# Expert matmuls over the 64 lower and the 64 upper output partitions, as two instructions each

## What is computed

```python
def body(acc, ws):
    wgu, wd, we = ws
    gu = x @ wgu                       # (tokens, 256) @ (256, 192)
    gate, up = jnp.split(gu, 2, axis=-1)
    act = jax.nn.silu(gate) * up       # (tokens, 96)
    out = act @ wd                     # (tokens, 96) @ (96, 256)
    return (acc + we[:, None] * out, None)
init = jnp.zeros_like(x)
final, _ = lax.scan(body, init, (gate_up_weights, down_weights, combine.T))
```

## Time and profile before

| what | value |
|---|---|
| time, median of 2 runs | 538.03 us (535.09 and 540.96) |
| span of the profiled execution | 534.3 us |
| TensorE busy | 478.1 us, 89% of the span |
| TensorE loads busy | 388.2 us, 73% |
| VectorE / ScalarE / GpSimd busy | 66% / 62% / 45% |
| chain that ended last | 61% TensorE, of it L1474 14%, L1494 9% |

### The profile page before, as it was taken

How to read it: one execution, slowest core, us unless ns; L and a number is a source line. 1 busy time by engine, 2 the same in 40 slices (tenths; PEclk the granted TensorE clock), 3 DMA queues, 4 the chain that set the end, 5 groups by cost and what they waited for, 6 DMA issues and landing times.

```text
span 534.3 us, 10363 instructions
## 1 busy us (share of the span) xinstructions
PE 478.1 (89%) x2751; PEld 388.2 (73%) x2751; DVE 352.2 (66%) x1175; ACT 332.2 (62%) x1021; POOL 238.5 (45%) x255
## 2 busy tenths in 40 slices
PE   3886999999989799999998647999999999999875
PEld 1466767887778777778875636889999898999621
DVE  5868488487398489479679744856666665666432
ACT  4556786888676879777987813555555555555400
POOL 0354102011012571101577777767667676765700
PEclk9899999999999999999999859999999999999989
DMA  7930992000030220300277246999999999993497
GB/s 274 421 130 20 301 334 85 1 1 1 2 80 10 73 76 10 76 2 0 82 269 275 91 150 187 368 400 399 400 393 388 397 396 398 385 366 131 150 354 250
DMA packets 71560, 108.54 MB, mean 203 GB/s; under 512 B 10234, under 2 KB 49351, under 8 KB 71120
## 3 DMA queue, kind: packets, MB, share of 16 engines
q1 hardware_dynamic: 62336, 90.93, 48.3%
q0 software_dynamic: 9168, 16.95, 8.7%
HBM read 81.31 MB, written 34.77 MB: 217 GB/s over the span
## 4 chain that ended last, share of the span: by engine, by line
PE 61%; DVE 14%; ACT 12%; DMA 6%; issue 4%; SPq 2%; POOL 1%; POOLq 0%; DVEq 0%; ACTq 0%
PE ps L1474 14%; PE ps L1214 10%; PE ps L1494 9%; PE ps L1339 7%; ACT lg L634 4%; DVE lg L912 3%; ACT lg L577 3%; PE ps L1262 2%; PE ps L1210 2%; PE ps L1212 2%; PE ps L1211 2%; PE ps L1255 2%; SPq L414 2%; PE ps L1320 2%; PE ps L1327 2%
## 5 line engine op out<-in xcount | busy, mean ns | idle before, releaser
L563 POOL DMA_INDIRECT pair_rows<-eout,dest x127 | 126.0, 992 | 54.9 <-DVE dest L1185 42.2
L1474 PE MATMUL ps<-wts,xg 128*128 128x192 f32 x508 | 105.0, 330 | 0.0
L1474 PEld LDWEIGHTS ps<-wts,xg 128*128 128x128 f32 x508 | 80.8, 193 | 0.1
L774 ACT ACTIVATE sact<-ps 128x96 f32<-128x96 f32 x127 | 31.9, 251 | 75.8 <-PE ps L1474 75.8
L1494 PE MATMUL ps<-wts,aT 96*128 96x256 f32 x254 | 76.0, 381 | 0.0
L1182 DVE COPY xg<-ps 128x256 f32<-128x256 f32 x127 | 53.9, 424 | 29.0 <-PE ps L1214 28.5
L634 ACT ACTIVATE lg<-lg,mneg 128x128 f32<-128x128 f32 (+1 forms) x128 | 56.4, 442 | 26.1 <-DVE mneg L912 26.1
L1195 DVE SCALAR_TENSOR_TENSOR aact<-sact,xrow,ps 128x96 f32<-128x96 f32 x127 | 39.9, 314 | 48.1 <-ACT sact L774 47.7
L483 POOL DMA_INDIRECT slot_rows<-rows,pair_slot x48 | 48.1, 1002 | 32.9 <-DVE hit L977 20.1
L577 ACT ACTIVATE eout<-ps 128x256 f32<-128x256 f32 x127 | 48.8, 384 | 17.2 <-PE ps L1494 1.2
L1214 PE MATMUL ps<-ident,xrow 128*128 128x128 f32 x254 | 50.1, 278 | 9.5 <-DMA xrow<-slot_rows 9.5
(11 more groups left out here) (220 smaller groups left out, 1043.3 us busy)
## 6 DMA issues: line engine op xcount, KB each, us to landing
wts<-in_experts_dram SPq DMA_DIRECT2D x127, 320.0 KB
xrow<-slot_rows SPq DMA_DIRECT2D x127, 130.0 KB, 7.9
slot_rows<-zero SPq DMA_DIRECT2D x1, 8320.0 KB, 28.3
pairs<-pair_rows SPq DMA_DIRECT2D x16, 512.0 KB
wT<-in_wq_t_dram SPq DMA_DIRECT2D x4, 512.0 KB, 6.8
wq_raw<-in_wq_l_dram SPq DMA_DIRECT2D x1, 2048.0 KB, 14.9
wo_sb<-in_wo_l_dram SPq DMA_DIRECT2D x1, 2048.0 KB, 20.7
bm<-bias_rows SPq DMA_DIRECT2D x4, 512.0 KB, 3.5
```

The lines of the kernel that those rows point to most:

```text
L563: nc.gpsimd.indirect_dma_start(out=pair_d, out_offset=bass.IndirectOffsetOnAxis(ap=dest[:, t:t + 1], axis=0), in_=eout[t % NOUT][:], in_of ...
L1474: ins = nc.tensor.matmul(ps[:, 2 + u % 2, 0:I2], xg[u % 3][:, cc, :], wts[u % NBUF][:, cc * I2:(cc + 1) * I2], start=(cc == 0), stop=(cc = ...
```

## The change

Each gate/up matmul and each down matmul becomes two. The first takes tokens 0 to 63 as the stationary operand and writes partitions 0 to 63 of the same bank, the second tokens 64 to 127 and partitions 64 to 127. Both have the same moving operand as before (192 or 256 columns). The built program marks each of them as working on an array part of 128 rows by 64 columns, at column 0 or 64, where before it was 128 by 128; the transposes keep 128 by 128. Nothing else is changed: waits, buffers and counts stay, and the last of the new instructions counts the semaphore.

```diff
                     for cc in range(CC):
-                        ins = nc.tensor.matmul(ps[:, 2 + u % 2, 0:I2], xg[u % 3][:, cc, :], wts[u % NBUF][:, cc * I2:(cc + 1) * I2],
-                                               start=(cc == 0), stop=(cc == CC - 1))
+                        for c0 in range(0, P, P // 2):
+                            ins = nc.tensor.matmul(ps[c0:c0 + P // 2, 2 + u % 2, 0:I2], xg[u % 3][:, cc, c0:c0 + P // 2],
+                                                   wts[u % NBUF][:, cc * I2:(cc + 1) * I2], start=(cc == 0), stop=(cc == CC - 1))
                     ins.then_inc(gu_done, 1)
...
-                    nc.tensor.matmul(ps[:, 6 + d % 2, 0:C], aT[d % 2][0:I, :], wts[d % NBUF][0:I, CC * I2:EW],
-                                     start=True, stop=True).then_inc(dn_done, 1)
+                    for c0 in range(0, P, P // 2):
+                        ins = nc.tensor.matmul(ps[c0:c0 + P // 2, 6 + d % 2, 0:C], aT[d % 2][0:I, c0:c0 + P // 2],
+                                               wts[d % NBUF][0:I, CC * I2:EW], start=True, stop=True)
+                    ins.then_inc(dn_done, 1)
```

## The result

The changed kernel takes 603.72 us (median of 2 runs, 602.92 and 604.53) against 538.03 before: a ratio of 1.121, 95% interval 1.114 to 1.128. The profiled execution has a span of 602.7 us, 68.4 more than the 534.3 of before.

A forecast was written before the change was run, and what follows sets the result against it. TensorE was taken as the bound; 127 tiles at + 0.60 us gave 76 us, less some 3 absorbed, so 607 us of span and, with 3.7 us to the median, 611 us; range 582 to 682.

The forecast's parts named there:

- What bounds the kernel: In the expert stage TensorE is the bound, busy 120.00 of 120.00 us at clock 1.00; transfers wait for it.
- Width of the stationary operand: In gate/up and down, a narrower stationary operand makes no pass cheaper: 0.163 us for 192 moving columns, 0.216 for 256.
- Loads of half the width: Loads of 64 columns in gate/up and down take 137 ns, stay hidden and cost zero; uncovered, 0.055 us a pass.
- I price the change of shape at zero: Four switches a tile between full transposes and narrow matmuls cost nothing, read from the 0.11 us around the `bneg` transpose.
- rival of the drain: Each of four shape changes a tile exposes 0.163 us: 694 us with halves overlapped, 755 without; chance 0.07.
- Overlap behind the load: In gate/up and down, the other half starts 0.055 us later, behind its load, in program order: + 0.60 us a tile.
- not slower: Halves of gate/up and down start out of program order, side by side, in 0.65 and 0.43 us: 538 us; chance 0.03.
- The sum: Over the expert stage 127 x 0.60 = 76 us, some 3 us absorbed: net + 73 us on the span of 534.3.
- the last step of the sum: From the profiled span of 607 us to the runs' median, 3.7 us higher: 611 us.
- What would show it wrong: Signs in the expert stage's chain: gate/up 0.98 us, down 0.70, a tile 2.01, transposes still 0.11; longer would be a drain.

The follow-up runs named there:

- the tiny matmuls: The kernel before with one tiny unread matmul ahead of each gate/up: 583.6 us with 64 tokens stationary, 560.6 us with 128 as control.
- quarters: Gate/up and down each split into four parts of 32 tokens instead of two of 64: 603.1 us, ratio 1.126 to the kernel before.
- grouped: The full split with TensorE's order changed so gate/up and down stand next to each other: 569.4 us, ratio 1.063 to the kernel before.

## Why the prediction was right in its number and wrong in its reasons

The time lies within the range of 582 to 682 and 7 us under the point of 611. Two steps of the working failed, in opposite directions and by nearly the same amount, so that the time was met by luck.

- **What bounds the kernel**: right. TensorE is busy throughout at clock 1.00 in both kernels, waits vanish after the first tiles, and every experiment's time follows its tile time to within some 10 us.
- **Width of the stationary operand**: right. 8 narrow passes without overlap took 0.64 us more than in pairs, which is 4 streams of the old price.
- **Loads of half the width**: right within a run of passes (they take 137 ns, as estimated, and the rounds of 0.163 us stay), wrong at a change of shape, where the first load starts with the step's first matmul and is laid bare, some 0.05 us (my own estimate for an uncovered load was 0.055).
- **"I price the change of shape at zero"**: the step that failed. The rows on `bneg` were of a transpose, which is compiled without a column group; they were no case of a change of shape, and I took them for one. Measured: 0.09 us of drain (the tiny matmuls, and the starts in the changed kernel), 0.14 to 0.15 with the bare load (in each of the chain's four steps), 0.59 a tile. My rival of the drain put it at 0.163 and gave it a chance of 0.07. The Trainium skill (TensorEngine Tiling (Array Packing), Key Properties) said that changing the mode drains the engine; the traces agree, with 0.09 us each time between full instructions and narrow matmuls.
- **"Overlap behind the load"**: the other step that failed, by + 0.60 us a tile where nothing was added. I held passes to the program's order and let each change of half wait for its load. The halves start in pairs, and even a pass four places later in the program does. This is the mechanism of my rival "not slower", to which I gave 0.03. The Trainium skill (TensorE: Matmul & The Clock Gate, Part 3 (packing small matmuls)) has the concurrency, which the traces show for f32 too (two passes 0.03 us behind a step's start, four with quarters). It also has starts in program order, which they contradict: with four lower passes ahead of the first upper one in the program, two passes still run 0.03 us behind the start.
- **The sum**: 0.60 a tile forecast and 0.59 measured, from other terms. With 0.59 x 127 = 75 us and a span that grew by 68.4, some 6.5 us were taken in somewhere, where I had taken off 3; the waits for rows shrank by only 1.9 us, and where the rest went stays open. Nearly another 3 us of the 7 under the point are in the last step of the sum: I added 3.7 us from the span to the median, and it was 1.0 this time.
- **What would show it wrong**: I had named 0.98 and 0.70 us for the two steps and 0.11 for a transpose. They read 0.80, 0.58 and 0.25. The profile said at once that the reasons were wrong, though the time was met.

No version here beats the kernel before: the best arrangement of the split (grouped) still has two changes a tile and 6% to pay, since the split saves nothing that a tile needs.

## What to carry to other kernels

Splitting a matmul over the columns of the array bought no time where the matmul already filled them; the parts only ran side by side to the old price, and each switch between full instructions and narrow matmuls cost 0.09 us plus the first load of the new shape. Where narrow matmuls are needed (few tokens), put those of one shape next to each other and count the switches, not the instructions. And take the price of an instruction from a row of its own kind: a row of a narrow transpose said nothing of a narrow matmul, and a look at the compiled instructions would have told that it was of another kind.

## What the runs showed that I had not expected

- Passes on other columns overtake at least three that stand ahead of them in the program; 16 passes of a quarter each take the same four rounds as 4 full ones (0.79 us with the changes of shape in it).
- A narrow f32 transpose is compiled as one without a column group, and neither drains nor loses its cover: 0.22 us with its full neighbour.
- Half of the surplus shows up where nothing was edited: the transposes went from 0.11 to 0.25 and from 0.22 to 0.37 us. What stands behind this drain in the engine, and why its 0.09 us is alike into the narrow shape and out of it, no run here tells.
